# Raw weights of experts four to eight loaded from ScalarE's DMA queue instead of SyncE's

## The reference, cut to what matters

```python
h = einsum('bhid,oi,od->bho', x, weighted_sum, weight)
h = h + attn(layernorm(h))            # 16 heads of 16, rope, unit q and k, softmax, out projection
z = layernorm(h)
w = sigmoid(z @ Wg + bg) * (sigmoid(...) > 0.5)       # (tokens, 8)
hid = relu(einsum('td,edh->eth', z, W1) + b1)         # 8 experts, hidden 1024
h = h + einsum('te,etd->td', w, einsum('eth,ehd->etd', hid, W2) + b2)
```

## Time and profile before

| quantity | value |
|---|---|
| median of 3 runs | 1963.07 us (1960.37 to 1966.18) |
| the profiled execution | 1957.52 us |
| its span, first to last instruction | 1955.7 us |
| PE busy | 1843.2 us (94%) |
| ACT busy | 1076.0 us (55%) |
| DVE busy | 746.4 us (38%) |
| POOL busy | 665.3 us (34%) |
| mean granted TensorE clock | 0.98 |
| DMA engines busy, mean of the one queue in use | 30.2% of 16 engines |

### The profile page before, as it was taken

The page is one execution under the profiler, slowest core; times in us unless marked ns, Lnnn a source line. Parts: engine busy times, 40 slices in busy tenths (PEclk is TensorE's granted clock), DMA queues, the critical chain, the costliest instruction groups (busy, mean ns, idle before and its releaser), DMA issues.

```text
span 1955.7 us, 31748 instructions
## 1 busy us (share of the span) xinstructions
PE 1843.2 (94%) x12608; PEld 1168.4 (60%) x12608; DVE 746.4 (38%) x1574; ACT 1076.0 (55%) x1649; POOL 665.3 (34%) x563
## 2 busy tenths in 40 slices
PE   5469789999999999999999999999999999999999
PEld 4137544676457754677546765477645775466666
DVE  5747844647004550146313371044601454032101
ACT  2455567545664466554665456654565546655444
POOL 1103332334333342334323243233433334234443
PEclk9689999999999999999999999999999999999999
DMA  4213453433213241231412233133412314122321
GB/s 160 65 65 115 128 184 112 177 98 103 92 66 118 88 130 65 87 119 66 129 66 89 98 100 114 47 113 112 110 64 97 119 58 126 65 87 98 108 90 52
DMA packets 109779, 194.54 MB, mean 99 GB/s; under 512 B 72616, under 2 KB 86464, under 8 KB 93248
## 3 DMA queue, kind: packets, MB, share of 16 engines
q1 hardware_dynamic: 109632, 192.51, 30.2%
HBM read 154.73 MB, written 20.98 MB: 90 GB/s over the span
## 4 chain that ended last, share of the span: by engine, by line
PE 74%; DVE 5%; DMA 4%; issue 2%; ACT 2%; SPq 0%; DVEq 0%; ACTq 0%
PE bank_h L870 28%; PE bank_f L889 10%; PE bank_f L892 9%; PE bank_f L891 9%; PE bank_o L798 5%; PE bank_s L784 4%; PE bank_s L715 2%; PE bank_s L716 2%; PE bank_s L717 2%; DMA qt<-probs 1%; DMA qt<-stack 1%; DMA raw<-in_w_dram 1%; DVE acc L1099 1%; PE bank_m L808 1%; DVE y L912 1%
## 5 line engine op out<-in xcount | busy, mean ns | idle before, releaser
L583 POOL TENSOR_TENSOR hl<-h,hh 128x512 f16<-128x512 f32 x512 | 599.9, 1172 | 1144.4 <-ACT hh L692 703.4
L870 PE MATMUL bank_h<-x,w1s 128*128 128x512 f16 x3072 | 751.0, 381 | 3.0 <-ACT hh L692 2.5
L689 ACT ACTIVATE h<-bank_h,b1s 128x512 f32<-128x512 f32 x512 | 351.2, 686 | 472.9 <-PE bank_h L870 471.4
L889 PE MATMUL bank_f<-w2s,hh 128*128 128x256 f16 x2048 | 561.4, 274 | 18.6 <-DVE acc L1099 18.6
L891 PE MATMUL bank_f<-w2s,hh 128*128 128x256 f16 x2048 | 559.8, 273 | 0.0
L892 PE MATMUL bank_f<-w2s,hl 128*128 128x256 f16 x2048 | 559.7, 273 | 0.0
L870 PEld LDWEIGHTS bank_h<-x,w1s 128*128 128x128 f16 x3072 | 288.0, 98 | 329.1 <-issue 39.4
L692 ACT ACTIVATE hh<-bank_h,b1s 128x512 f16<-128x512 f32 x512 | 349.8, 683 | 0.0
L658 ACT ACTIVATE probs<-bank_s 128x1024 f32<-128x1024 f32 x240 | 246.5, 1027 | 185.0 <-PE bank_s L784 183.9
L889 PEld LDWEIGHTS bank_f<-w2s,hh 128*128 128x128 f16 x2048 | 201.6, 98 | 127.3 <-issue 62.4
L1099 DVE SCALAR_TENSOR_TENSOR acc<-bank_f,gw,acc 128x256 f32<-128x256 f32 x256 | 106.1, 477 | 367.8 <-PE bank_f L892 367.5
(11 more groups left out here) (135 smaller groups left out, 1509.2 us busy)
## 6 DMA issues: line engine op xcount, KB each, us to landing
w1s<-w_parts SPq DMA_DIRECT2D x56, 1024.0 KB, 4.8
w2s<-w_parts SPq DMA_DIRECT2D x56, 1024.0 KB, 4.8
xraw<-in_x_t_dram SPq DMA_DIRECT2D x32, 512.0 KB, 5.2
raw<-in_w_dram SPq DMA_DIRECT2D x16, 1024.0 KB, 6.4
w_parts<-w1s SPq DMA_DIRECT2D x8, 1024.0 KB, 8.7
w_parts<-w2s SPq DMA_DIRECT2D x8, 1024.0 KB, 11.7
out_dram<-acc SPq DMA_DIRECT2D x16, 256.0 KB, 6.0
turned_gates<-maxima_rows SPq DMA_DIRECT2D x6, 192.0 KB, 3.3
```

Of the source, the lines that this page charges most:

```text
L583: pool.tensor_tensor(hl[n % HBUFS][:], h32[n % 2][:], hh[n % HBUFS][:], ALU.subtract)\
L689: act.activation(h32[n % 2][:], bank_h[n % 2][:, :], ACT.Relu, bias=b1s[:, e, m:m + 1]).then_inc(h_hi.sem, 1)
L870: last = pe.matmul(bank_h[n % 2][:, :], w[:, wp, k, m * P:(m + 1) * P], x16s[fb % 2][:, xp, k, :], start=(k == 0 and wp + xp == 0), stop=( ...
L889: pe.matmul(o, high, w[:, 0, m, :], start=(m == 0 and t % 2 == 0), stop=False, skip_group_check=True)
```

## The change

The five raw loads for e = 3 to 7 leave SP's list. In ACT's list two new stages stand for each: "raw_w1" 0.6 chunks after the second piece of w1 (the fifth entry of the table), and "raw_w2" 0.5 chunks after the last piece. Each waits for the same count of `parts_lo` as SP did and then issues the same transfer from ACT. Loads for e = 0, 1 and 2 stay on SP.

```diff
         stages += [("parts", PIECES * e + p) for p in range(PIECES)]
-        prep += [(start + at, *stage) for at, stage in zip(early if e == 2 else late, stages)]
+        at_parts = early if e == 2 else late
+        prep += [(start + at, *stage) for at, stage in zip(at_parts, stages)]
+        if e + 1 < EXPERTS:
+            prep += [(start + at_parts[4] + 0.6, "raw_w1", e + 1), (start + at_parts[6] + 0.5, "raw_w2", e + 1)]
...
             for e in range(2, EXPERTS):
                 if e == 3:
                     turn_stacks(1, range(TT))
-                if e + 1 < EXPERTS:
-                    load_raw(e + 1)
                 store_parts(e)
                 if e + 1 < EXPERTS:
                     share_maxima(e + 1)
...
+                elif stage == "raw_w1":
+                    act.wait_ge(parts_lo, PIECES * (n - 1) + PIECES // 2)
+                    act.dma_start(raw[:, 0:2048].rearrange("p (k n) -> p k n", k=DK),
+                                  w1[n].rearrange("(k p) n -> p k n", p=P)).then_inc(raw_in[0], 16)
+                elif stage == "raw_w2":
+                    act.wait_ge(parts_lo, PIECES * n)
+                    act.dma_start(raw[:, 2048:4096].rearrange("p (k n) -> p k n", k=HM),
+                                  w2[n].rearrange("(k p) n -> p k n", p=P)).then_inc(raw_in[1], 16)
```

## The result

The changed kernel takes 1972.33 us (median of 7 runs, 1968.01 to 1975.77), beside 1963.26 us for the kernel before (7 runs, 1960.37 to 1966.18). The ratio is 1.0044, with a 95% interval of 1.0030 to 1.0057: slower by 9.1 us. A second measurement with five rounds gave 1969.40 against 1962.69 us, 1.0036 (1.0023 to 1.0049). The forecast was 1970 us with a range of 1960 to 1977, and its sum was +7.3 us. The size of the whole was right, but the terms were not; that is the subject of what follows.

The account below looks back on a forecast made before the run. Before 400 us, what ends last at PE's three large idle times was taken to bound the kernel. Terms 2.5 + 0.4 + 1.3 + 3.1 = +7.3 us, against the 1963.07 us median, gave 1970 us, range 1960 to 1977.

Parts of the forecast that it names:

- C and D: Sixth and seventh expert's loads: ACT's stalls delay exponentials that PE waits for, later w2 does not matter; +1.3 us.
- E: Eighth expert's load: w2 lands 4.9 us later beside the stores, 1.8 won back on the maxima's store; +3.1 us.
- B: Fifth expert's loads, PE's wait until 256.48: w1 goes earlier, but w2 ends last, near the stores; +0.4 us.
- A: Fourth expert's loads, PE's wait until 222.37: ACT's two waits delay DVE, the bound there; +2.5 us.
- The issue on ACT: Each of the ten raw-load issues on ACT was taken to cost 0.45 us, between 0.3 and 1.28.
- Rival 3: ACT's issues cost 1.28 us instead of 0.45, some 4 us more in all, 1974 us; chance 0.12.
- Rival 2: Fifth expert's early load pays: PE's 5.28 us wait shrinks to 1.7, clock stays up, -5.6 us there; chance 0.18.
- Equal shares: Assumed split of DMA time between w2 load and two stores: w2 ends with them, 4.9 us later at the eighth expert.
- PE's first idle: Sign of right: PE's 6.51 us idle until 222.37, at the fourth expert's loads, grows to near 9 us.
- PE's third wait: Sign of right: PE's 3.06 us wait until 363.93, at the eighth expert, grows to near 6 us.
- PE's wait at 256 for the addition: Sign of wrong if gone: PE's 5.28 us wait until 256.48 for DVE's addition, at the fifth expert.
- Rival 1: The second queue gives w2 an even or better share of bytes; sum +3.7 us, 1964 to 1967 us; chance 0.30.

Follow-up runs that it names:

- first pair: Changed kernel's profile against the first profile of the kernel before, span 14.8 us longer; the other pair takes the second measurement of each, 5.1 us longer.
- act_last3: Kernel before with only the sixth to eighth expert's raw loads issued from ACT; 1967.13 us against 1962.22, ratio 1.0026.
- act_fifth: Kernel before with only the fifth expert's raw loads issued from ACT; 1959.48 us against 1962.22, ratio 0.9986.
- before_stores_late: Kernel before, loads still on SP, with the stores issued behind the exchange of the next expert's maxima; 1957.25 us against 1962.69, ratio 0.9975.
- waits_only: Changed kernel with ACT's ten waits kept but no DMA on ACT, SP issuing the loads as before; 1965.30 us against 1962.69, ratio 1.0013.
- fifth_stores_late: Kernel before with late stores and only the fifth expert's raw loads issued from ACT; 1955.83 us against 1962.11, ratio 0.9973.
- after_again: The changed kernel measured a second time, unaltered; 1969.40 us against 1962.69 for the kernel before, ratio 1.0036.
- all_but_fifth: Changed kernel with the fifth expert's raw loads left on SP, the other four experts' on ACT; 1969.33 us against 1962.11, ratio 1.0040.
- before_again: The kernel before, unaltered, run as if it were a changed one; 1961.86 us against 1962.69, ratio 0.9997.
- act_fourth: Kernel before with only the fourth expert's raw loads issued from ACT; 1963.78 us against 1962.22, ratio 1.0006.
- after_stores_late: Changed kernel with the stores issued behind the exchange of the next expert's maxima; 1963.35 us against 1962.22 for the kernel before, ratio 0.9999.

## Why the prediction came out right, and which steps did not

**The forecast, 0.37% slower, was right; measured were 0.44 and 0.36%.** The three causes had the right sign, but the nearness of the sum is in part luck. The term for C and D was less than half of what it should be; in the first pair the sum fell short by that and by E, and in the second a gain at B cancelled it. B and E moved by 2 to 3 us between two pairs of profiles, which no single sum can hit.

- **A, +2.5: nearly right.** 2.0 to 2.3 in the five profiles that have these loads on ACT. ACT's stands were forecast at about 2.6 and 2 us and were 3.11 and 2.89, the issue included. DVE's were forecast at 1.7 (195.1 - 193.40) and 0.9 to 1.0 and came to 1.73 and 0.99. What I set too low was the give-back: of the 0.9 us by which the first w2 piece was too long I took back 0.2, and it lost all of them.
- **The issue on ACT, 0.45 us: right.** It took 0.37 to 0.42 us. Rival 3, dear issues of 1.28 us, fell.
- **B, +0.4: right in size, wrong in content.** +1.4 and -1.5 in the two pairs. I had w2 landing among the stores and PE waiting for the addition. In fact the raw loads held up the last transposes, which the forecast named nowhere as at risk, PE waited for those, and SP issued the stores only at 252.99, when w2 (landed 253.35) was nearly in. Rival 2's 5.6 us were never there, because the stall it removes has a transpose's behind it.
- **C and D, +1.3: the step that failed.** It said that the w2 load lands later "but DVE's addition there waits for PE, not for the load". Behind the late load the addition does make PE wait (0.47 us at 296.24). And the addition is not the only one that needs the load: ACT's first cast needs the scales, and it stands ahead of an exponential in ACT's list. A load 5 us late pushed that cast, the exponential and PE, and in the first pair the clock fell on top. Measured +3.9 and +3.2, +3.5 in act_last3.
- **E, +3.1: mechanism right, terms around it mis-sized.** Equal shares gave w2 4.9 us of lateness, 1.1 of it the later issue, with a landing 10.6 us after the issue. Measured in the first pair, with the shift that is carried along taken off: 4.6 us, 1.0 of it the later issue, and a landing after 10.34. That term was right. Too large was the 1.8 us taken back: the maxima's store gave 1.4, but the way back lost 1.1 of it, and a DVE instruction in the chain took 0.9 more. No row gave the "about 1 us ahead of its first byte", the only thing that parts equal shares from w2 coming last in this sum. The clock, which the forecast left out, made 1.5 us of difference between the pairs.
- **Signs.** Of the signs named for "right", ACT's two stands and w2 landing over 8 us after its issue came. PE's first idle, forecast near 9 us, was 5.86: PE had already stood 2.33 us instead of 1.18 at an earlier qkv step, so the lateness was there and the long wait was not. PE's third wait, near 6 us, came as two, 2.81 and 3.05. One sign of "wrong" came too: PE's wait at 256 for the addition was gone, for the reason given at B.
- **Shares of the queues.** The stores land in a median of 4.8 and 8.3 us and the w2 load beside them in 10.4, so it comes last of three transfers whose issues begin within 0.5 us. Equal shares would have had it end together with the second store or ahead of it; the order of landings speaks against them, though the time of the landing came out nearly as they gave it. Rival 1, an even or better share, fell. The prediction also named a sum near +9 if w2 came last; the two measurements are +9.1 and +6.7. The Trainium skill, page "DMA: Bandwidth & Descriptors", section "Queues, rings and completion order", says that a DMA engine goes round the queues that have work and takes a packet, typically of 9 to 17 descriptors, from one before it goes to the next. An estimate from this: the w2 load moves pieces of 1 KB (128x8x256 in float32) and a store pieces of 8 KB (128x4096 in float16), so the stores' queue would move more bytes in its turn. The order of landings above agrees; the turns themselves are in no trace here, and no run changes the size of the pieces.

**Left open.** Why act_fifth gains 2.7 us in the medians while its profile shows 0.65 at B, and why that gain is absent from the whole change. No run tells why the w2 load comes last in the other queue: the size of its pieces is the one cause named, and it was not varied. Which part of a transpose (issue or data) the load beside it delays: both got longer together, 1.28 to 4.35 us for an issue, 3.2 (median) to 6.95 us for a landing, and no run took them apart.

## What to carry to other kernels

A queue is also an order. Here the latency-critical load stood ahead of 2 MB of stores that nobody waited for, and a queue of its own took that protection away: 10.3 us instead of 6.7. Its lateness then went through two engines' lists, since DVE's maxima and ACT's cast each stand ahead of something that PE needs. Before moving a load to another engine, ask what it had been ahead of, and first try to issue the bulk behind it, which alone gave 0.25% here. And a wait put into a busy engine's list holds up all that follows; if the engine that sets the pace needs one of those, its loss is the kernel's.

## What the runs showed of the hardware

- The issue of a 1 MB load on ACT takes 0.37 to 0.42 us of its list (the ten of the changed kernel).
- DMA transposes suffer from a plain load beside them: the issue of `kt` goes from 1.28 to 3.55 and 4.35 us, and the landing of `qt` to 6.13 and 6.95 us from a median of 3.2. Two 1 MB stores do the same in before_stores_late (issues of 3.06 and 4.30 us). ACT's waits without the loads do not (1.23 to 1.29 us in waits_only).
- A 1 MB w2 load lands in 5.3 to 5.6 us when it is alone, in 6.7 with two stores behind it in its own queue (8.3 to 10.5 at the fifth expert, with w1's load directly ahead as well), and in 10.3 to 11.8 with the same stores in another queue.
- An idle time of PE of 1.7 to 4.4 us is sometimes followed by the 1.2 GHz level and sometimes not. At PE's last wait at E the clock stayed up through 1.72, 1.98, 2.58, 2.79 and 3.05 us (before_stores_late, fifth_stores_late, after_again, all_but_fifth, act_last3). It was down by the next matmul after 3.05, 3.06, 3.54, 3.81 and 4.38 us (the changed kernel, the kernel before, before_again, act_fourth, waits_only), and it fell about 1 us into the work after 2.39 and 3.79 us (after_stores_late, act_fifth). So the length of the wait alone does not settle it.
